# Gate and up of the FFN as seven block products in place of eight, over pairs of batches

## The reference, cut to what matters

```
x = x + attn(_layernorm(x), w_attn, b_attn, w_proj, b_proj)
h = _layernorm(x)
gate = silu(einsum('bsh,ih->bsi', h, w_gate))     # 4 x 512 tokens, 512 -> 1376
up   = einsum('bsh,ih->bsi', h, w_up)
x = x + einsum('bsi,hi->bsh', gate * up, w_down)  # 1376 -> 512
```

## Time and profile before

| what | value |
|---|---|
| runs | median 870.93 us of 3 (870.82 to 875.95) |
| profiled execution, own time | 872.66 us |
| its span | 871.0 us, mean granted clock 0.983 |
| FFN block on TensorE | 517.64 us to about 866.5 us |
| PE busy | 814.4 us, 94% |
| DVE / ACT / POOL busy | 501.1 / 356.9 / 186.0 us |

### The profile page before, as it was taken

The page is one execution under the profiler, slowest core; times in us unless marked ns, Lnnn a source line. Parts: engine busy times, 40 slices in busy tenths (PEclk is TensorE's granted clock), DMA queues, the critical chain, the costliest instruction groups (busy, mean ns, idle before and its releaser), DMA issues. The chain is left out here.

```text
span 871.0 us, 13365 instructions
## 1 busy us (share of the span) xinstructions
PE 814.4 (94%) x4576; PEld 562.1 (65%) x4576; DVE 501.1 (58%) x1539; ACT 356.9 (41%) x693; POOL 186.0 (21%) x336
## 2 busy tenths in 40 slices
PE   1989899999999999999988989999999999999998
PEld 1745355556555565555633668887888788878886
DVE  6498877877988789887884444342222312232223
ACT  4336656665566655666556333231111211121111
POOL 5213333342433424334233300000000000000000
PEclk9999899999999999999988999999999999999999
DMA  8683645655565565665742337004000400030001
GB/s 273 173 261 110 177 139 196 196 158 187 193 211 186 155 190 188 207 195 154 240 146 82 117 123 263 13 1 146 0 1 1 145 0 0 0 131 13 0 0 48
DMA packets 70563, 109.31 MB, mean 126 GB/s; under 512 B 13395, under 2 KB 38662, under 8 KB 70505
## 3 DMA queue, kind: packets, MB, share of 16 engines
q1 hardware_dynamic: 68457, 108.32, 38.7%
q10 hardware_dynamic: 2048, 0.27, 0.2%
HBM read 65.97 MB, written 42.32 MB: 124 GB/s over the span
## 5 line engine op out<-in xcount | busy, mean ns | idle before, releaser
L903 DVE CUSTOM_DVE_ANT_0 bank<-bank,mask_qk 128x512 f32<-128x512 f32 (+3 forms) x512 | 240.1, 513 | 53.9 <-PE bank L1132 51.5
L737 ACT ACTIVATE pt<-bank 128x512 f32<-128x512 f32 (+1 forms) x384 | 194.0, 529 | 136.3 <-PE bank L1154 123.6
L1154 PE MATMUL bank<-q_st,k_st 116*128 116x512 bf16 (+3 forms) x512 | 134.4, 306 | 13.9 <-ACT pt L737 12.1
L1473 DVE TENSOR_TENSOR gu<-bank,silu 128x512 f32<-128x512 f32 x40 | 27.7, 692 | 199.5 <-issue 120.0
L1132 PE MATMUL bank<-k_st,q_st 97*128 97x512 bf16 (+3 forms) x512 | 131.5, 307 | 9.2 <-DVE mx L903 4.2
L1251 PE MATMUL bank<-fT_hi,wgu_hi 128*128 128x512 f32 x224 | 88.0, 393 | 4.1 <-DVE wgu_lo L1443 4.1
L1132 PEld LDWEIGHTS bank<-k_st,q_st 97*128 97x128 bf16 x512 | 41.0, 98 | 77.6 <-issue 36.6
L1251 PE MATMUL bank<-fT_lo,wgu_hi 128*128 128x512 f32 x224 | 87.6, 391 | 0.0
L1251 PE MATMUL bank<-fT_hi,wgu_lo 128*128 128x512 f32 x224 | 87.6, 391 | 0.0
L1406 ACT ACTIVATE silu<-bank 128x512 f32<-128x512 f32 x40 | 23.9, 598 | 147.6 <-PE bank L1251 147.6
L1171 PE MATMUL bank<-pt,v_nat 128*32 128x512 f32 (+3 forms) x1024 | 81.6, 463 | 2.8 <-POOL pt L646 2.1
(11 more groups left out here) (106 smaller groups left out, 1394.6 us busy)
## 6 DMA issues: line engine op xcount, KB each, us to landing
stack_dram<-scratch SPq DMA_DIRECT2D x32, 384.0 KB, 3.1
q_st<-stack_dram SPq DMA_DIRECT2D x32, 384.0 KB
k_st<-stack_dram SPq DMA_DIRECT2D x32, 384.0 KB
stack_dram<-scratch SPq DMA_DIRECT2D x32, 256.0 KB, 3.2
pv_dram<-weighed SPq DMA_DIRECT2D x32, 256.0 KB, 4.5
weighed<-pv_dram SPq DMA_DIRECT2D x17, 256.0 KB
xt<-x SPq DMA_DIRECT2D x16, 256.0 KB, 3.9
stack_dram<-scratch SPq DMA_DIRECT2D x32, 128.0 KB, 3.9
```

The costliest lines, as they stand in the source:

```text
L737: act.activation(pt[:, h % PT_RING, COL0[k]:COL0[k] + WIDE[k]], bank[3 + (3 * h + k) % 2][:, 0:WIDE[k]], ACT.Exp, scale=1.0 / HD).then_inc ...
L903: last = dve.tensor_tensor_reduce(bank[k][:, at:at + n], bank[k][:, at:at + n], mask_qk[:, S - n:S], 1.0, NEG, ALU.add, ALU.max, mx[:, h % ...
L1154: last = pe.matmul(bank[3 + u % 2][:, at:at + n], k_st[0:K_EXP, s, h % 4, t * P:(t + 1) * P], q_st[0:K_EXP, s, h % 4, t * P:S], start=True ...
L1473: dve.tensor_tensor(gu[:, f % 2, :], bank[5 + 2 * (f % 2)][:, :], silu[:, f % 2, :], ALU.mult).then_inc(gu_done, 1)
```

## The change

Take two batches A (even) and B (odd), and split the 512 values of a token in two halves. For one slice, gate and up of A and B are the product of a 2x2 block matrix of weights (gate and up by the two halves) and a 2x2 block matrix of tokens (the two halves by A and B): eight block products, each of 2 contraction blocks x 3 = 6 matmuls. The change computes the same four results by Winograd's scheme with seven block products. It needs four sums of weight blocks, (`S1` to `S4`), four combinations of token blocks (`T1` to `T4`), and seven additions of 128x512 afterwards.

- A slice of a pair of batches is a **unit**: seven products P1, P2, P6, P5, P7, P3, P4, in this order, of 6 matmuls each, and between them the four quarters of one down slice of an earlier unit (`unit`). There are 17 units: slices 5 to 10 of batches 0 and 1, all 11 of batches 2 and 3. Tiles that stay plain: slice 4 of batch 0, slices 0 to 4 of batch 1 (`tile`).
- The down slices that no unit takes along come in a row at the end of each pair (`END`), 12 after the units of a pair, counting the one held back. In the first pair the two rounds of transposes for batches 2 and 3 stand between them, and VectorE makes the token combinations of the second pair there.
- Weights of gate and up are not kept: each unit loads its 512 KB, GpSimd makes the four sums (`weight_sums`), ScalarE casts 3 + 4 blocks of 128x256, VectorE makes their low parts, one unit ahead, into two buffers. Weights of down are loaded again for every down slice (44 in place of 11), into a ring of 3; ScalarE casts them and GpSimd, not VectorE, makes the low part.
- VectorE has per unit: seven additions from PSUM, two products with a silu, the low parts of the next weights (512, 256 and 1024 columns) and of one product; ScalarE a copy of P1, two silus, the casts. The additions of one unit read the banks which the next products take: there are four banks for the products, so P7 of a unit waits for the second addition.
- Layer norm statistics of batches 2 and 3 stand in units 1 and 2, normalising in units 2 and 3, on VectorE between the second and the third addition.
- All loops are unrolled.

The diff, cut to its core:

```diff
...
-    RAW = 3
+    RAW, RAW_DOWN, GU, WD = 2, 3, EARLY, 4
+    PLAIN = EARLY + 1
+    TILES = [(0, EARLY)] + [(1, f) for f in range(PLAIN)]
+    UNITS = [(0, f) for f in range(PLAIN, FT)] + [(1, f) for f in range(FT)]
+    FIRST = FT - PLAIN
+    DOWNS = [(0, f) for f in range(FT - 1)] + [(1, 0), (0, FT - 1)] + [(1, f) for f in range(1, FT)]
+    DOWNS += [(b + 2, f) for b, f in DOWNS]
+    PAIR = 2 * FT
+    BEHIND = {u: EARLY + u for u in range(FIRST)} | {u: PAIR + u - FIRST - 1 for u in range(FIRST + 1, len(UNITS))}
+    END = {FIRST - 1: FT, len(UNITS) - 1: PAIR + FT}
+    DOWN_BANK = ((0, 1, 2, 3), (7, 6, 4, 5), (4, 5, 6, 7), (2, 1, 3, 0))
...
+    P1, P2, P6, P5, P7, P3, P4 = range(7)
+    def product_bank(u, j):
+        return bank[4 + (7 * u + j) % 4] if u < FIRST else bank[(7 * (u - FIRST) + j) % 4]
...
+            for u in range(len(UNITS)):
+                if u in BEHIND:
+                    load_down(BEHIND[u] + 2)
+                load_gate_up(RAW + 1 + u)
+                if u == 0:
+                    sp.wait_ge(c_lo, 4)
+                    load_tokens(2)
+                    for s in x1_stored:
+                        sp.wait_ge(s, B * TT // 2 * 16)
+                    load_tokens(3)
+                if u in END:
+                    n, b = END[u], UNITS[u][0] * 2
+                    for i in range(n + 1, n + 4):
+                        load_down(i)
+                    store(b)
+                    for i in range(n + 4, n + 7):
+                        load_down(i)
+                    load_residual(b + 1)
+                    for i in range(n + 7, n + FT + 2):
+                        load_down(i)
+                if u == FIRST:
+                    store(1)
+                if u == FIRST + 2:
+                    load_residual(2)
...
+            def weight_sums(u):
+                if u >= len(UNITS):
+                    return
+                need(pool, w_lo_done, 2 * u)
+                pool.wait_ge(raw_in[(u + 1) % RAW], 16 * ((u + 1) // RAW + 1))
+                raw = wgu_raw[(u + 1) % RAW]
+                s = {o: weight_sum[:, o - S1, :, :] for o in (S1, S2, S3, S4)}
+                a11, a12, a21, a22 = raw[:, 0, 0:2, :], raw[:, 0, 2:4, :], raw[:, 1, 0:2, :], raw[:, 1, 2:4, :]
+                pool.tensor_tensor(s[S1], a21, a22, ALU.add).then_inc(sum_step, 1)
+                pool.tensor_tensor(s[S3], a11, a21, ALU.subtract).then_inc(sum_step, 1)
+                pool.wait_ge(sum_step, 3 * u + 1)
+                pool.tensor_tensor(s[S2], s[S1], a11, ALU.subtract).then_inc(sum_step, 1)
+                pool.wait_ge(sum_step, 3 * u + 3)
+                pool.tensor_tensor(s[S4], a12, s[S2], ALU.subtract).then_inc(sums_made, 1)
+            def down_lo(n):
+                if n < len(DOWNS):
+                    pool.wait_ge(wd_hi_done, n + 1)
+                    pool.tensor_tensor(wd_lo[:, n % WD, :], wd_raw[:, n % RAW_DOWN, :], wd_hi[:, n % WD, :].bitcast(F32),
+                                       ALU.subtract).then_inc(wd_lo_done, 1)
...
+            for u in range(len(UNITS)):
+                weight_sums(u + 1)
+                if u in (2, 3):
+                    deviation(u)
+                if u in BEHIND:
+                    down_lo(BEHIND[u] + 1)
+                if u == FIRST:
+                    down_lo(PAIR)
+                if u in END:
+                    for n in range(END[u], END[u] + FT):
+                        down_lo(n)
...
+            def weights_hi(u):
+                if u >= len(UNITS):
+                    return
+                if u < 2:
+                    act.wait_ge(tile_done, 2 * (3 + 2 * u))
+                else:
+                    act.wait_ge(product_done, 7 * (u - 1))
+                act.wait_ge(raw_in[(u + 1) % RAW], 16 * ((u + 1) // RAW + 1))
+                raw, hi = wgu_raw[(u + 1) % RAW], place(w_hi, u)
+                act.copy(hi[:, A11:A12 + 1, :, :].rearrange("p o k m -> p (o k) m"), raw[:, 0, :, :])
+                act.copy(hi[:, A22, :, :], raw[:, 1, 2:4, :]).then_inc(w_hi_done, 1)
+            def weight_sums_hi(u):
+                if u >= len(UNITS):
+                    return
+                act.wait_ge(sums_made, u + 1)
+                act.copy(place(w_hi, u)[:, S1:S4 + 1, :, :], weight_sum[:, :, :, :]).then_inc(w_hi_done, 1)
...
+            for u in range(len(UNITS)):
+                pair, f = UNITS[u]
+                act.wait_ge(product_done, 7 * u + P1 + 1)
+                need(act, summed, 7 * u - 5)
+                act.copy(p1, product_bank(u, P1)[:, :]).then_inc(copied, 1)
+                act.wait_ge(summed, 7 * u + 1)
+                act.activation(gates[:, 0, :], gates[:, 0, :], ACT.Silu).then_inc(silu_done, 1)
+                weights_hi(u + 1)
+                if u in BEHIND:
+                    down_hi(BEHIND[u] + 1)
+                if u == FIRST:
+                    down_hi(PAIR)
+                weight_sums_hi(u + 1)
+                if u in END:
+                    down_hi(END[u])
+                    product_hi(END[u] - 1)
+                act.wait_ge(summed, 7 * u + 6)
+                act.activation(gates[:, 1, :], gates[:, 1, :], ACT.Silu).then_inc(silu_done, 1)
+                product_hi(DOWNS.index((2 * pair, f)))
+                if u in END:
+                    for i in range(FT - 1):
+                        down_hi(END[u] + 1 + i)
+                        product_hi(END[u] + 1 + i)
+                        if pair == 0 and i in (3, 5):
+                            transposed_round((i - 3) // 2)
+                        if pair == 0 and i == 7:
+                            combination_hi(1, T1, 2)
+                            combination_hi(1, T3, 3)
+                        if pair == 0 and i == 8:
+                            combination_hi(1, T2, 4)
+                            combination_hi(1, T4, 6)
...
+            def combination_lo(pair, j, count):
+                dve.wait_ge(c_hi, 4 * pair + count)
+                dve.tensor_tensor(cT_lo[:, j, :, :], cT[j], cT_hi[:, j, :, :].bitcast(F32),
+                                  ALU.subtract).then_inc(c_lo, 1)
+            def weights_lo(u):
+                if u >= len(UNITS):
+                    return
+                dve.wait_ge(w_hi_done, 2 * u + 1)
+                raw, hi, lo = wgu_raw[(u + 1) % RAW], place(w_hi, u).bitcast(F32), place(w_lo, u)
+                dve.tensor_tensor(lo[:, A11:A12 + 1, :, :].rearrange("p o k m -> p (o k) m"), raw[:, 0, :, :],
+                                  hi[:, A11:A12 + 1, :, :].rearrange("p o k m -> p (o k) m"), ALU.subtract)
+                dve.tensor_tensor(lo[:, A22, :, :], raw[:, 1, 2:4, :], hi[:, A22, :, :], ALU.subtract).then_inc(w_lo_done, 1)
+            def weight_sums_lo(u):
+                if u >= len(UNITS):
+                    return
+                dve.wait_ge(w_hi_done, 2 * u + 2)
+                hi, lo = place(w_hi, u).bitcast(F32), place(w_lo, u)
+                dve.tensor_tensor(lo[:, S1:S4 + 1, :, :], weight_sum[:, :, :, :], hi[:, S1:S4 + 1, :, :],
+                                  ALU.subtract).then_inc(w_lo_done, 1)
...
+            for u in range(len(UNITS)):
+                pair, f = UNITS[u]
+                p = [product_bank(u, j) for j in range(7)]
+                if u == FIRST:
+                    add_residual(1)
+                dve.wait_ge(product_done, 7 * u + P2 + 1)
+                dve.wait_ge(copied, u + 1)
+                dve.tensor_tensor(gates[:, 0, :], p[P2][:, :], p1, ALU.add).then_inc(summed, 1)
+                weights_lo(u + 1)
+                dve.wait_ge(product_done, 7 * u + P6 + 1)
+                dve.tensor_tensor(u2, p[P6][:, :], p1, ALU.add).then_inc(summed, 1)
+                if u in (2, 3):
+                    normalised(u)
+                if u in (1, 2):
+                    token_statistics(u + 1)
+                dve.wait_ge(product_done, 7 * u + P5 + 1)
+                dve.wait_ge(summed, 7 * u + 2)
+                dve.tensor_tensor(u4, p[P5][:, :], u2, ALU.add).then_inc(summed, 1)
+                weight_sums_lo(u + 1)
+                dve.wait_ge(product_done, 7 * u + P7 + 1)
+                dve.tensor_tensor(u2, p[P7][:, :], u2, ALU.add).then_inc(summed, 1)
+                dve.wait_ge(summed, 7 * u + 4)
+                dve.tensor_tensor(up_odd, p[P5][:, :], u2, ALU.add).then_inc(summed, 1)
+                dve.wait_ge(product_done, 7 * u + P3 + 1)
+                dve.tensor_tensor(gates[:, 1, :], p[P3][:, :], u4, ALU.add).then_inc(summed, 1)
+                if u in END:
+                    product_lo(END[u] - 1)
+                dve.wait_ge(silu_done, len(TILES) + 2 * u + 2)
+                dve.tensor_tensor(gu_odd[:, f, :], gates[:, 1, :], up_odd, ALU.mult).then_inc(odd_done, 1)
+                dve.wait_ge(product_done, 7 * u + P4 + 1)
+                dve.tensor_tensor(u2, p[P4][:, :], u2, ALU.add).then_inc(summed, 1)
+                dve.wait_ge(summed, 7 * u + 7)
```

(84 more changed lines are left out.)

490 lines of the change are left out of this document (272 added, 218 removed).

## The result

The changed kernel takes **884.67 us** (median of 4 runs, 882.68 to 886.68) against 871.64 us (4 runs, 870.82 to 875.95) before it in the same job: a ratio of 1.0125, with an interval of 1.0097 to 1.0152. So it is slower by 1.3%. I had forecast 865, with a range up to 884. What came is the second rival, at its price of 883.

The account below looks back on a forecast made before the run. TensorE was taken as the bound, busy 94% of 871.0 us. Less 28.4 us of removed work gives 842.6; plus 22.4 us of waits on the VectorE and ScalarE loop gives 865 us, range 851 to 884.

Parts of the forecast that it names:

- Rival 2: GpSimd's operations hold up VectorE's weight remainders and products in each unit: 1.3 us x 14 = 18, 883 us; chance 0.15.
- Removed work: 102 gate and up matmuls, a transpose round, loop restarts and a late last addition go: 28.4 us, leaving 842.6.
- a VectorE that is not idle gets in first: In every unit, GpSimd was taken to work in VectorE's gaps: 0 us lost, upper bound its whole 3.9 us per unit.
- (a): Units 1 to 3: statistics and normalising of batches 2 and 3 in VectorE's chain, 11.0 us less slack: 8 us.
- (b): End of the first pair: VectorE's combinations, splits and remainders make the last down slice late: 6 us.
- From P2 to P7: Each of 12 plain units: path through ScalarE and VectorE takes 7.09 us against TensorE's 6.80; 0.3 each, 3.6 us.
- (c): First unit of the second pair: four residual additions before its first sum, no down quarters as cover: 2.7 us.
- (d): Handover at both pair ends: down slice wants the even product just made and waits for finished sums: 2.1 us.
- The prologue: First weights and first tile after attention keep their price, batch 1's token work is covered: 0 us extra.
- rival 4: Stalls of 2 to 3 us around units 2 to 4 bring half clock, 4 x 1.7 us: 872 us; chance 0.10.
- Rival 1: FFN waits hidden, TensorE stays the bound: 842.6 to 852, say 847 us; chance 0.15.
- Rival 3: Loads queued behind stores come late at pair ends (two x 3 us) and prologue (2 us): 873 us; chance 0.12.

Follow-up runs that it names:

- Experiment 10: Experiment 7 with GpSimd's weight sums and down remainders made for one column only, the rest zeros; 847.89 us, FFN stage 325.08 us.
- experiment 1: Changed kernel with ScalarE casting the down weights' high part before the first silu, not after the next unit's weights; 867.17 us, ratio 0.995.
- experiment 8: Changed kernel with VectorE's weight remainder of 256 columns put before that of 512, nothing else; 867.58 us, ratio 0.9945.
- experiment 2: Changed kernel with GpSimd's weight sums and down remainders on one column only, results not the layer's; 860.34 us, FFN stage 337.68 us.
- Experiment 4: Changed kernel without statistics and normalising of batches 2 and 3, but for short operations that keep the order; 877.87 us, ratio 1.0062.
- Experiment 7: Changed kernel with earlier down cast, second sum before weight remainders, product remainders before combinations at first pair's end, statistics and normalising spread over units; 851.0 us, ratio 0.9762.

## Why the prediction was wrong, step by step

**Removed work: right.** The counts came as predicted (102 matmuls and 16 transposes fewer). Experiment 10, which takes GpSimd out of the way, comes within 3.9 us of the sum for TensorE's work.

**The step that failed: "a VectorE that is not idle gets in first", and so 0 us for the meetings.** I took it from the earlier trace rows, where a GpSimd operation issued during a run of three VectorE operations took 1.37 us. I then costed the meetings at 0 above what (a) and (b) hold. In the changed kernel GpSimd, issued 0.04 us before VectorE's next operation, gets the port for its whole length in 16 of 16 such meetings. Experiments 1 and 8 remove that meeting in two independent ways and give 16.3 and 16.1 us; experiment 2 puts all meetings at up to 25.0. With no port the sum of the prediction would be 343.6 less some 4 for the GpSimd time in (a) and (b), 339.6; experiment 2 measured 337.7. So without GpSimd the rest of the sum holds to 2 us, some of its terms too high and others too low (below), and this one step carries nearly all of the 19.1: 3.1 of it are the two stretches at half clock, which I had also put at nothing, and which are gone in experiment 2, where no wait behind the first tile is over 1.94 us.

The trace of the kernel before had a second such row, which the prediction does not use:

```profile
472.10 0.49 DVE L933 SCALAR_TENSOR_TENSOR aT_lo<-weighed,bias_qkv,aT_hi 128x256 fp32r<-128x256 f32 x1 [1.26 <-ACT aT_hi L753]
472.40 0.44 POOL L650 TENSOR_SCALAR_AFFINE_SELECT pt<-pt 128x256 f32<-128x256 f32 x1 [0.26 <-ACT pt L737]
472.50 0.89 DVE L957 TENSOR_TENSOR w_lo<-xt,w_hi 128x512 fp32r<-128x512 f32 x1
```

VectorE is in a run of operations here too, GpSimd is issued 0.10 us before the next one, runs its usual 0.44, and line 957 takes 0.89 in place of 0.67. So one row spoke for the step and one against it. My other row was read too strongly as well: the 1.15 us of line 933 in the earlier trace rows are to be set against the 0.58 that this line takes in the median of its 32 instances, not against the 0.41 of another line.

Behind it lies an argument on averages. I wrote that the weight sums are released as VectorE turns to sums that read PSUM, and leave it free for about 2.6 us. That is nearly true of the weight sums. But the large operation, the down remainder, is released by ScalarE's cast, which stands right behind the next unit's weight casts (lines 1521, 1522) in ScalarE's order. It is therefore issued 0.57 us after line 1661 starts, in each of these 16 units. The order of the three engines was in the code; lining them up would have put the meeting between lines 1661 and 1663.

**From P2 to P7, 0.3 us in each plain unit: a little too high without the meeting, 1.26 with it.** In experiment 1 TensorE waits for 0.12 us of 110, so the path was shorter than I had it. The meeting adds 1.11 us to one link (1.53 in place of 0.42) and the gap before P7 is 0.95, so the path has under 0.2 us of slack, and that is why the link shows almost in full.

**(a) Statistics, 8 us: right.** Experiment 4 has 7.6. Experiment 7 shows that most of it was a matter of place.

**(b) Combinations, 6 us: about right.** The four gaps before down slices at the pair's end are 1.63, 1.25, 2.27 and 1.68 us, 6.8 together, but part of it is the port: lines 1631, 1635 and 1644 take 2133, 1921 and 1967 ns, and line 1631's operation 1226 alone. **(c) First unit of pair 1, 2.7 us: too low**, with gaps of 0.66, 2.46 and 1.05, 4.2 together. **(d) Handovers, 2.1 us: too high**, 0.47 and 0.55.

**The prologue, 0 us: too low by 1.2.** The first 24 matmuls take 8.37 us against 7.17 in the earlier trace rows; the granted clock is 0.69 from 514.84 to 524.00.

**What I left out.** Two things, summed from TensorE's timeline from start to start. The first is the half clock behind waits: two stretches, 3.1 us (rival 4, below). The second is that the matmuls just behind a wait are slow at the full clock too: the first is followed after 0.34 us and not 0.23, and a few others after 0.3. The stage has 26 gaps of over half a microsecond, and these small delays come to about 5 us. The ledger then closes: gaps of 12.1 us before P7 in 14 units, 7.6 in the units with statistics, 6.8 and 4.2 from (b) and (c), 1.0 from (d), 0.4 elsewhere, 1.2 of the prologue, 3.1 at half clock and these 5 make 41.4 of the measured 41.5.

**The rivals.** Rival 1 (waits hidden, 847) is what the change can be: experiment 7 is at 851.0. Rival 2 came true in its mechanism: it had half a meeting of 1.3 us and half of two of 0.66, 1.3 us a unit, on top of the 0.3 from P2 to P7; measured 1.26 with everything. That the total came within 2 us of 883 is partly luck, as the half clock and the small delays fill what the units fell short of. The weights within it were different: one whole meeting with the down remainder, and little from the weight sums, of which the last runs into the odd product (line 1741, mean 890 ns against 692 in experiment 2). I gave it 0.15, against a forecast of 0.48 that rested on one row of two. Rival 3 (transfers) did not come: no wait of TensorE in the list ends in a transfer. ScalarE does wait for down weights,

```profile
ACT wd_hi L1492 <- DMA wd_raw<-w_down: 23.8, 6, 6.4
```

but at times when it is ahead. Rival 4 (clock) came by half, and I had written that no half clock would show after the first tile. The granted clock is 0.50 from 595.6 to 599.0 and from 704.8 to 708.2, in a unit with the statistics and in the first unit of the second pair, beginning 0.4 and 0.8 us after TensorE resumed from gaps of 2.2 and 2.5 us:

```profile
595.25 0.48 PE L1823 MATMUL bank<-wd_hi,w_hi 128*128 128x512 f32 x1 [2.01 <-DVE w_lo L1623]
595.95 0.63 PE L1823 MATMUL bank<-wd_hi,w_lo 128*128 128x512 f32 x1
596.38 0.63 PE L1251 MATMUL bank<-cT_hi,w_hi 128*128 128x512 f32 x1
```

It cost 3.1 us where the rival had 6.8. My reason against it, that such gaps are shorter than the 4 us before the first tile, did not hold; but gaps of 2.1 us before 612.73 and 2.3 before 687.99 were not followed by it, and what decides is not shown here.

**What stays open.** In the earlier trace rows GpSimd's operation was issued 0.09 us before VectorE's next one and lost; in the changed kernel it is issued 0.04 us before and wins, 16 times of 16. The first was a select on one input and the second a subtraction of two inputs, but that does not decide by itself: the row at 472.40 is a select too, issued 0.10 us before, and wins. The point within VectorE's running operation does not sort them simply either (0.52 us into it in the row that lost, 0.30 and 0.57 in those that won). Why came out the other way, no run here tells.

## What to carry to other kernels

Where two engines can lock each other out, a mean of busy time says nothing: write down, for one period, what releases each operation of either, and see which pairs fall together, the longest first. If the path has less slack than one such operation, move its release to where the other engine reads PSUM or waits; here that was one line of ScalarE's order, or two instructions of VectorE's swapped, for 16 us. And a single row in which one side wins is no rule: such a cost belongs in the sum at a whole meeting per period until a row shows the same pair of operations. Where a change adds waits of 2 us to TensorE, count the half clock behind some of them too.

## What the runs showed of the hardware

- **The one issued first has it in these cases, by hundredths of a microsecond.** GpSimd 0.04 us ahead: VectorE's 256 columns take 1.53 us in place of 0.42. GpSimd 0.23 us behind: it is GpSimd that waits, 1.61 for 1.29, and VectorE's line 1662 is not held up (0.68 or 0.69 in all 17). The Trainium skill (SBUF — State Buffer, Who interferes with whom) says that whoever issues first gets the shared pair for the whole instruction, and that issue order decides who blocks; the trace agrees in these two cases and in the row at 472.40, and the earlier trace rows is the one that I can't fit.
- **A VectorE operation that reads one input from PSUM is not held up** by GpSimd: 0.68 us beside a GpSimd operation of two SBUF inputs (line 1723 in experiment 8).
- **GpSimd's narrow operations are dearer than their share.** A subtraction or sum of 128x256 took 0.81 to 0.85 us on average in the changed kernel (0.74 in the clear) where 128x512 takes 1.29; my estimate was 0.66.
- **A wait costs TensorE more than its gap.** At the full clock the first matmul behind it is followed after 0.34 us and not 0.23, and twelve take 2.86 us from start to start and not 2.72.
- **A wait of a little over 2 us can be followed by half clock.** Behind two gaps of 2.2 and 2.5 us the granted clock was 0.50 for 3.4 us, about 1.6 us lost each; behind gaps of 2.1 and 2.3 us it was not.
- **The same code does not end at the same time.** The attention part, unchanged, ends anywhere from 511.93 to 520.29 us in the twelve profiles; a stage has to be measured by its own ends.
